# Attention masks added as packed bytes once a batch, eight score tiles held, and the tables that order five engines rewritten

## The reference, cut to what matters

```python
# x (4, 512, 512), ctx (4, 512, 128), attn_mask (512, 512) bool, pad_mask (4, 512) bool
def attention(ctx, attn_mask, pad_mask, qc, Wq, bq, Wk, bk):
    qp = einsum('bsh,oh->bso', ctx, Wq) + bq
    kp = einsum('bth,oh->bto', ctx, Wk) + bk
    scores = einsum('bsh,bth->bst', qp, kp) * 128 ** -0.5 * qc
    mask = attn_mask[None, :, :] | pad_mask[:, None, :]
    return softmax(where(mask, -inf, scores))

def qlinear(x, w):                      # weights to -1, 0, 1; rows of x to 8 bits
    ws = mean(abs(w)) + 1e-5;  wq = clip(round(w / ws), -1, 1)
    xs = max(abs(x), axis=-1) / 127 + 1e-5;  xq = clip(round(x / xs), -128, 127)
    return einsum('bsi,oi->bso', xq, wq) * xs * ws

x = x + tanh(g_xattn) * attention(ctx, attn_mask, pad_mask, layernorm(x), Wq, bq, Wk, bk)
h = layernorm(x)
x = x + tanh(g_ffn) * qlinear(silu(qlinear(h, w_gate)) * qlinear(h, w_up), w_down)   # 512 -> 2048 -> 512
```

## Time and profile before

| what | value |
|---|---|
| median of 3 runs | 228.04 us |
| the profiled execution's own time | 227.88 us |
| its span, first to last instruction | 226.1 us |
| PE busy | 201.0 us (89%), 854 matmul rows |
| DVE busy | 175.3 us (78%) |
| ACT busy | 131.5 us (58%) |
| POOL busy | 127.7 us (56%) |

### The profile page before, as it was taken

One profiled execution on the slowest core, in us unless ns is written; L12 is line 12 of the kernel. 1 busy time (PEld: TensorE's weight loads), 2 busy tenths in 40 slices (PEclk: granted clock), 3 DMA queues, 4 the chain that ended last, 5 costly groups with the idle time before them and its releaser, 6 DMA issues.

```text
span 226.1 us, 2874 instructions
## 1 busy us (share of the span) xinstructions
PE 201.0 (89%) x854; PEld 90.8 (40%) x854; DVE 175.3 (78%) x343; ACT 131.5 (58%) x173; POOL 127.7 (56%) x180
## 2 busy tenths in 40 slices
PE   8714526979999998999999999999999999999994
PEld 7201104234444443444444444444444444444441
DVE  0588897899879899699969889897998675786221
ACT  2559986965989410466994305977655525771400
POOL 2898799999999998225168775117994000000000
PEclk9985555799999999999999999999999999999999
DMA  6999979865004466204235632414846626001982
GB/s 222 422 420 417 417 282 372 311 188 226 0 0 93 96 139 117 70 0 96 46 77 108 139 96 72 89 27 94 112 76 117 162 49 139 3 0 20 202 198 93
DMA packets 47360, 32.84 MB, mean 145 GB/s; under 512 B 40944, under 2 KB 41072, under 8 KB 45808
## 3 DMA queue, kind: packets, MB, share of 16 engines
q1 hardware_dynamic: 47200, 32.51, 50.9%
q10 hardware_dynamic: 144, 0.13, 0.3%
HBM read 18.48 MB, written 4.19 MB: 100 GB/s over the span
## 4 chain that ended last, share of the span: by engine, by line
PE 59%; POOL 23%; issue 7%; DVE 4%; DMA 4%; ACT 1%; SPq 0%; POOLq 0%; DVEq 0%
PE pD L978 20%; PE pU L962 19%; PE pG L949 18%; POOL down_w L548 3%; POOL mask_bias L467 2%; POOL up_w L548 2%; PE pA L926 2%; POOL x L504 2%; DMA hid<-in_masks 2%; POOL probs L517 2%; DVE x L1265 2%; POOL gate_w L548 2%; POOL probs L501 2%; DMA xqT<-xq 1%; POOL esd L512 1%
## 5 line engine op out<-in xcount | busy, mean ns | idle before, releaser
L747 ACT ACTIVATE hid<-pG,act_g 128x512 f32<-128x512 f32 x64 | 43.7, 686 | 52.9 <-PE pG L949 52.3
L949 PE MATMUL pG<-gate_w,xqT 128*128 128x512 f16 x256 | 65.0, 387 | 1.7 <-DMA xqT<-xq 1.0
L962 PE MATMUL pU<-up_w,xqT 128*128 128x512 f16 x256 | 62.1, 379 | 1.1 <-DVE up_w L1355 1.1
L978 PE MATMUL pD<-down_w,stage_b 128*128 128x512 f16 x256 | 57.9, 379 | 0.2 <-DMA stage_b<-stage_b 0.2
L1312 DVE TENSOR_TENSOR hid<-pU,hid 128x512 f32<-128x512 f32 x64 | 43.7, 685 | 13.3 <-PE pU L962 11.7
L754 ACT ACTIVATE stage_b<-hid,inv 128x1024 f16<-128x1024 f32 x32 | 35.7, 1141 | 16.1 <-DVE inv L1330 10.4
L949 PEld LDWEIGHTS pG<-gate_w,xqT 128*128 128x128 f16 x256 | 25.2, 99 | 38.0 <-issue 8.9
L962 PEld LDWEIGHTS pU<-up_w,xqT 128*128 128x128 f16 x256 | 24.9, 98 | 31.3 <-DVE up_w L1355 1.2
L978 PEld LDWEIGHTS pD<-down_w,stage_b 128*128 128x128 f16 x256 | 25.0, 98 | 30.6 <-issue 0.6
L555 POOL TENSOR_SCALAR out_scale<-den,act_e,down_k 128x1 f32<-128x1 f32 x16 | 5.4, 339 | 42.2 <-DVE den L1327 42.2
L467 POOL TENSOR_TENSOR mask_bias<-attn_bias,pad_bias 128x512 bf16<-128x512 bf16 x16 | 18.8, 1178 | 8.0 <-DVE mx L1249 7.8
(11 more groups left out here) (86 smaller groups left out, 232.1 us busy)
## 6 DMA issues: line engine op xcount, KB each, us to landing
stage_a<-in_L_ffn_w_gate SPq DMA_DIRECT2D x4, 1024.0 KB, 10.8
stage_b<-in_L_ffn_w_up SPq DMA_DIRECT2D x4, 1024.0 KB, 19.3
stage_a<-in_L_ffn_w_down SPq DMA_DIRECT2D x4, 1024.0 KB, 6.1
stage_b<-in_x SPq DMA_DIRECT2D x2, 1024.0 KB, 6.0
out<-x SPq DMA_DIRECT2D x8, 256.0 KB, 2.5
out<-stage_b SPq DMA_DIRECT2D x8, 256.0 KB, 2.4
ctx_s<-in_ctx SPq DMA_DIRECT2D x4, 256.0 KB, 5.7
x<-in_x SPq DMA_DIRECT2D x2, 512.0 KB, 7.8
```

What stands on the lines that cost most here:

```text
L747: act.activation(hid[:, t % NH, n * 512:(n + 1) * 512], pG[c % NG][:, :], ACT.Silu, scale=act_g[:, t:t + 1]).then_inc(silu_done, 1)
L949: ins = pe.matmul(pG[c % NG][:, :], xqT[:, t // TILES % 2, t % TILES, k, :], gate_w[:, n, k, :], start=k == 0, stop=k == KD - 1)
L962: ins = pe.matmul(pU[c % NU][:, :], xqT[:, t // TILES % 2, t % TILES, k, :], up_w[:, n, k, :], start=k == 0, stop=k == KD - 1)
L978: ins = pe.matmul(pD[t % ND][:, :], hidT[:, t % 2, k, :], down_w[:, k // KD, k % KD, :], start=k == 0, stop=k == KI - 1)
```

## The change

- **Masks.** The bytes stay bytes. `mask(b)` adds, once a batch, the four tiles' attention mask and the batch's padding mask, read as 32-bit words: 128 partitions x 512 words, on POOL. The four conversion passes are gone; 16 additions become 4. `mask_and_max` takes the byte tile as its second input, and computes score x 2^30 - byte. So that one byte is enough to mask, the queries are scaled by 2^-80 and the row scale is made to match. The bytes now have a buffer of their own, and silu(3, 0) no longer waits for the conversions.
- **Buffers.** `probs` holds 8 tiles (`NP`), so that `score(t)` waits for tile t - 8. Contexts, queries and keys hold 3 batches (`NQ`); the loads of contexts 2 and 3 now stand ahead of the second x batch in SP's list.
- **Bank.** The first transposes use pD[1] in place of pA. `transpose_x(1)` then waits for the first copy, and `down(1, 0)` for both.
- **Order.** The lists of PE, DVE, ACT, POOL and SP are written anew.
- The memory kept for software-made DMA descriptors is cut to 1024.

```diff
+NQ, NP = 3, 8
...
-MASKED = -1.5e35
+SMALL = 2.0 ** -80
+BACK = 2.0 ** 30
+V1 = (SMALL * BACK) ** 2
+MASKED = -0.5 * BACK
...
-        pA16 = pA[:, :].bitcast(F16).rearrange("p (k t) -> p k t", t=P)
+        pX16 = pD[1][:, :].bitcast(F16).rearrange("p (k t) -> p k t", t=P)
...
+            def mask(b):
+                if b == 0:
+                    pool.wait_ge(mask_loaded, 16)
+                if b >= 2:
+                    pool.wait_ge(masked, TILES * (b - 1))
+                w = S // 4
+                pad = masks_i32[:, (TILES + b) * w:(TILES + b + 1) * w].rearrange("p (j w) -> p j w", j=1)
+                pool.tensor_tensor(mask_i32[b % 2].rearrange("p (j w) -> p j w", w=w),
+                                   masks_i32[:, 0:TILES * w].rearrange("p (j w) -> p j w", w=w),
+                                   pad.broadcast_to([P, TILES, w]), ALU.add).then_inc(mask_ready, 1)
...
-                act.activation(qT[:, b % 2, :], pA[:, :], ACT.Identity, scale=SCALING, bias=bqs[:, :])\
+                act.activation(qT[:, b % NQ, :], pA[:, :], ACT.Identity, scale=SCALING * SMALL, bias=bqs[:, :])\
...
-                    if t == NH - 1:
-                        act.wait_ge(bias_made, 4)
...
+                if p:
+                    pe.wait_ge(xqT_ready, p)
...
+                        if t == 1:
+                            pe.wait_ge(xqT_ready, TRANSPOSE_BY.count("P"))
...
-                if t >= TILES:
-                    quantised_x(dve, t - TILES)
-                dve.scalar_tensor_tensor(probs[:, t % TILES, :], xt(t), mv1[:, t, 0:1], bank[:, :],
+                if t >= NP:
+                    quantised_x(dve, t - NP)
+                dve.scalar_tensor_tensor(probs[:, t % NP, :], xt(t), mv1[:, t, 0:1], bank[:, :],
...
-                dve.tensor_tensor_reduce(probs[:, t % TILES, :], probs[:, t % TILES, :], mask_bias[:, t % 2, :],
-                                         1.0, NEG, ALU.add, ALU.max, mx[:, t:t + 1]).then_inc(masked, 1)
+                b, j = divmod(t, TILES)
+                dve.wait_ge(mask_ready, b + 1)
+                dve.tensor_tensor_reduce(probs[:, t % NP, :], probs[:, t % NP, :], mask_u8[:, b % 2, j * S:(j + 1) * S],
+                                         BACK, NEG, ALU.subtract, ALU.max, mx[:, t:t + 1]).then_inc(masked, 1)
...
+            transpose_x(0)
+            gate(0, 0)
+            gate(1, 0)
+            weight_sum(1)
+            gate(0, 1)
+            gate(1, 1)
             pe.wait_ge(scored, 5)
-            transpose_x(0)
-            weight_sum(1)
-            gate(0, 0)
-            pe.wait_ge(xqT_ready, 1)
             score(5)
-            gate(1, 0)
+            transpose_x(1)
+            gate(0, 2)
             pe.wait_ge(scored, 6)
             score(6)
-            gate(0, 1)
+            gate(1, 2)
+            pe.wait_ge(scored, 7)
+            score(7)
```

More of the change, by code:

```diff
@@ L599, in _ @@
-            quantise_x(2)
-            gate_scales(1)
-            quantise_x(3)
             up_scales(1)
             weight_round(1, 2)
-            mask(8)
+            exp_bias(2)
+            mask(3)
             weight_round(1, 3)
-            exp_bias(2)
             weight_round(2, 0)
-            mask(9)
             weight_round(2, 1)
+            valid_sums(2)
             weight_round(2, 2)
-            valid_sums(2)
+            residual1(4)
+            scale_out(0)
+            residual1(5)
@@ L612, in _ @@
+            centre(4)
+            residual1(6)
+            centre(5)
+            std2(2)
             weight_round(2, 3)
-            scale_out(0)
-            residual1(4)
-            residual1(5)
+            quantise_x(4)
             scale_out(1)
-            residual1(6)
-            centre(4)
+            quantise_x(5)
+            gate_scales(2)
             residual1(7)
-            scale_out(2)
-            std2(2)
-            centre(5)
-            std2(3)
+            up_scales(2)
@@ L640, in _ @@
+            valid_sums(3)
             scale_out(4)
-            mask(13)
-            rstd(4)
-            valid_sums(3)
             residual1(8)
-            scale_out(5)
             residual1(9)
             residual1(10)
+            scale_out(5)
+            residual1(11)
             centre(8)
-            scale_out(6)
+            rstd(4)
             std2(4)
             centre(9)
-            residual1(11)
+            quantise_x(8)
             gate_scales(4)
-            quantise_x(8)
+            quantise_x(9)
@@ L672, in _ @@
             centre(12)
+            residual1(14)
+            residual1(15)
             scale_out(9)
@@ L824, in _ @@
             silu(6, 2)
-            quantise_hidden(4, 0)
+            silu(6, 3)
             exp(8)
@@ L1107, in _ @@
             down(5, 1)
+            pe.wait_ge(scored, 12)
+            score(12)
+            up(6, 2)
+            up(6, 3)
+            pe.wait_ge(scored, 13)
+            score(13)
             down(5, 2)
+            down(5, 3)
             up(7, 0)
@@ L1111, in _ @@
             up(7, 2)
+            pe.wait_ge(scored, 14)
+            score(14)
+            gate(8, 0)
             up(7, 3)
-            down(5, 3)
+            up(8, 0)
+            gate(8, 1)
+            gate(8, 2)
             down(6, 0)
@@ L1433, in _ @@
             absmax_hidden(1, 1)
-            weight_bound(2, 3)
+            absmax_x(5)
+            score(8)
+            inverse_x(2)
+            inverse_std2(2)
             product(2, 1)
             inverse_hidden(1)
+            mask_and_max(8)
+            weight_bound(2, 3)
+            product(2, 2)
+            score(9)
+            residual2(0)
+            mask_and_max(9)
+            stats2(6)
             absmax_hidden(2, 0)
-            product(2, 2)
-            stats2(4)
+            absmax_x(6)
@@ new lines, in _ @@
+            absmax_hidden(3, 0)
+            mask_and_max(10)
+            reciprocal_scale(3)
+            product(3, 2)
+            stats1(11)
+            product(3, 3)
+            score(11)
+            product(4, 0)
+            mask_and_max(11)
+            product(4, 1)
+            absmax_hidden(3, 1)
+            product(4, 2)
+            absmax_hidden(4, 0)
+            product(4, 3)
+            inverse_hidden(3)
+            absmax_hidden(4, 1)
+            product(5, 0)
+            residual2(1)
@@ L1494, in _ @@
-            product(6, 0)
-            absmax_hidden(5, 1)
+            stats2(9)
+            absmax_x(8)
             product(6, 1)
-            gate_sums(3)
-            inverse_hidden(5)
-            residual2(3)
+            residual2(4)
+            absmax_hidden(6, 0)
+            inverse_std2(4)
+            absmax_x(9)
+            score(12)
             product(6, 2)
-            absmax_hidden(6, 0)
+            mask_and_max(12)
+            inverse_x(4)
             product(6, 3)
-            stats2(8)
+            score(13)
@@ L1520, in _ @@
+            product(7, 1)
+            reciprocal_scale(4)
+            absmax_hidden(7, 0)
+            product(7, 2)
+            score(14)
+            product(7, 3)
+            mask_and_max(14)
+            absmax_hidden(7, 1)
+            product(8, 0)
+            inverse_hidden(7)
+            stats2(10)
             stats2(11)
+            residual2(6)
             absmax_x(10)
-            score(13)
-            residual2(6)
-            mask_and_max(13)
+            inverse_std2(5)
+            score(15)
```

702 lines of the change are left out of this document (306 added, 396 removed).

## The result

| | kernel before | with the change |
|---|---|---|
| median | 228.04 us (227.93 to 228.21, 5 runs) | 229.22 us (229.08 to 229.32, 5 runs) |
| ratio, 95% interval | | 1.0043 (1.0027 to 1.0059) |
| span of the profiled execution | 226.1 us | 227.2 us |
| its last part after PE's last matmul | 3.2 us | 3.2 us |
| loss (end of PE's last matmul less 187.7 us of work) | 35.2 us | 36.3 us |

A forecast was written before the change was run, and what follows sets the result against it. PE was taken as the bound, its 35.2 us loss arising almost wholly before 50 us. The replay's 30.3 plus 0.9 for contention gave 31.2, so -4.0 us and 224.0 us, range 222.4 to 227.0.

The forecast's parts named there:

- What bounds the kernel: Whole kernel: PE's 35.2 us loss; only what fills PE before 50 us, and one 1.0 us wait, can change the time.
- Masks: POOL's mask work: integer addition taken at 1.27 us, POOL losing 17.9 us of work; byte-input mask_and_max taken at 0.69 us.
- rival 2: POOL's four mask additions: integer addition is slow and the change loses; 229.6 us at 3 us each; chance 0.07.
- Start: Masks through first weight scale: DVE reaches weight_scale(0) 1.5 us earlier, first rounding at 24.1 instead of 25.61.
- Bank: First transposes: with their own bank PE no longer waits 5.8 us for DVE's score(4); gate(0, 0) at 33.1, not 37.39.
- Contexts ahead of an x batch, costed at nothing: Early loads: x tiles 4 to 7 arrive at 33, DVE asks at 33.8; without that cover up to 1 us.
- Tile 4 and the later stages: PE reaches gate(4, 0) at 77.5, its transpose ready at 76 to 76.7; the end keeps the same 3.2 us.
- Rival 3: After the early stretch: gain spent later, as tiles 4, 8 or 12 come late by 4 us in all; 228; chance 0.06.
- What the undisturbed durations leave out: DVE and POOL between 26 and 75 us: steps stretched by contention, 0.9 us added to the loss.
- The replay of the lists: New lists stepped at profiled durations: up(0, 0) at 46.5, up(0, 3) at 56.3, loss 30.3 us.
- Rival 1: DVE's queue from 40 to 75 us takes half back, 2 us beyond the 0.9 reaching PE: 226.0 us; chance 0.20.

The follow-up runs named there:

- b_bank: b_masks plus a bank of its own for the first transposes and the few step moves it needs: 223.71 us (0.9808); again on another chip 224.66 us (0.9847).
- b_masks: The kernel before with the byte masks alone, rings, bank and other order as they were: 225.12 us, ratio 0.9864.
- b_rings: b_bank plus 8 score tiles, contexts, queries and keys of 3 batches, and contexts 2 and 3 loaded ahead of the second x batch: 225.42 us, 0.988.
- a_halves: The changed kernel with each weight rounding on POOL split into two instructions of 1024 columns: 227.93 us, ratio 0.9984.
- a_up1: The changed kernel with sums, scale, first rounding and first chunks of the up weights moved forward in the lists: 228.32 us, ratio 1.0005.
- a_cut: The changed kernel with the statistics of x tiles 4 to 7 over 64 columns instead of 512, 2.3 us less DVE work: 228.55 us, 1.0003.

## Why the prediction was wrong

- **What bounds the kernel:** right. All that counted was what fills PE before about 60 us; the end is as it was (3.2 us). The clock was back before 43 us.
- **Masks:** right. The integer addition takes 1.27 us, the value taken; rival 2 is out. POOL lost 20.4 us (17.9 by additions and passes and 3.4 by shorter roundings; other steps grew by 0.9). `mask_and_max` with a byte input takes 0.69 us where it is alone. By itself the part gives 3.1 us.
- **Start:** the first rounding at 24.56 (24.1). Nearly right.
- **Bank:** right in kind: with it `b_bank` stands at 0.9808 and 0.9847 where `b_masks` stands at 0.9864, so it is worth 0.4 to 1.3 us in the old lists (the lower figure isn't told from nothing). In the changed kernel the wait of 5.8 us became 2.5 for ACT and 3.4 for the copy.
- **Contexts ahead of an x batch, costed at nothing:** wrong in the old lists. The cover named there is gone in `b_rings` (2.32 us of waiting in the trace; the 0.3% on the time is within the intervals). The changed kernel wasn't run without the early contexts.
- **Tile 4 and the later stages:** right. `gate(4, 0)` starts at 83.11 without a wait; the predicted 77.5 is off by what was lost ahead of it. Rival 3 is out.
- **"What the undisturbed durations leave out", 0.9 us:** this is the step that failed. It counted five masks and a residual that are stretched by 1.2 us each, "most of it beside a wait", and no `weight_bound` at all: in the kernel before that step took 0.69 us for gate, 0.90 for up, and looked immune. In part that was because DVE stood there waiting when the rounding ended. In the new lists DVE never waits there, and seven of the twelve begin inside a step of POOL and are stretched. The bill on the bounds is 7.1 us more than before, up to 1.7 us a time, on the very steps that release PE: 1.63 us ahead of the first copy; 1.67 (a `mask_and_max`) and 0.75 ahead of `up(0, 0)`; 1.6 and 1.4 ahead of `up(0, 3)`. Taking the rounding's "undisturbed" 2.17 from a pair hid the same thing: the trace of the kernel before has roundings of 1.97, and one of the pair was stretched. A replay with durations from a trace carries the old order's collisions into the new order.
- **What the runs put in its place:** by `up(0, 3)` the changed kernel had lost 5.3 us more than the replay. `a_halves` gives 3.2 of them back there, against the 0.9 allowed; 1.3 reach the end. What caused the other 2.1 stays open.
- **The replay of the lists:** `gate(0, 0)` is 2.0 us late, the first up rounding 1.9, `up(0, 0)` 2.9, the end of the fourth up rounding 3.1 (56.64, not 53.5), `up(0, 3)` 5.3. So the last 2.2 us arise on DVE: after that rounding it still had the rest of a stretched bound, two products and a `TENSOR_REDUCE` of 1.20 us before it came to the bound that PE wanted, at 59.42.
- **Rival 1** (DVE's queue takes half back) named the right engine: it put 2 us beyond the 0.9 on it, of 5.2 missed, by an average stretch of which a third reaches PE.

Of the lists' 3.7 us, then, 1.3 to 1.5 are accounted for by runs that gave them back. What the other 2.2 us or more are made of stays open: earlier up weights gave 0.9 in `a_up1` and less work for DVE 0.9 in `a_cut` (neither has a clean sum with the halves), ACT's order gave nothing. That so many gate chunks, clipped one by one, stand in front of the first up chunk is argued from `b_bank`'s 42.12 against 49.38, and no run put the order of `b_bank` into the changed kernel step by step.

Why did the change not pay, then? Its masks and bank are worth 1.5 to 1.9% in the old lists, its rings cost about 0.3% (within the intervals), and its new lists 1.6%.
